# Attention and feed-forward kernel: the mark above a threshold as the upper byte of bf16, without the constant pass

## The chip, the cores and the metric

The kernel runs on one core of a Trainium2 chip. The metric is device time in microseconds (us) of that core for the whole program, the median of several runs. Engines are TensorE (PE, with PEld for its weight loads), VectorE (DVE), ScalarE (ACT), GpSimd (POOL) and SyncE (SP, which issues DMAs).

## What is computed

`x` has shape (16, 512, 256). The layer is attention with 16 heads of width 16, in which each row of scores keeps its 31 largest entries, then a layer norm, then a gated feed-forward layer of width 768 with integer weights, then a second layer norm. Cut to what matters:

```python
scores = einsum('bhqd,bhkd->bhqk', Q, K) / sqrt(16)
top_vals, _ = top_k(scores, 31)
scores = where(scores < top_vals[..., -1:], -inf, scores)
context = einsum('bhqk,bhkd->bhqd', softmax(scores), V)
x = layernorm(x + context @ Wo.T + bo)
h = silu(x @ wg.T) * (x @ wu.T)
x = layernorm(x + h @ wd.T)
```

## The kernel before, in words

The work goes batch by batch, and within a batch in 64 slots. A slot is one tile of scores, 128 queries of one head against 512 keys. Every engine has its own program, `slots`, which runs over n = 0 to 63 and does in slot n one step of each of several tiles at once; constants at the head of the file say how many slots behind the scores a step runs (`COUNT0 = 1`, `COUNT1 = 2`, `BELOW = 4`, `BLOCK = 5`, `SORT = 6`, `PICK = 14`, `THRESHOLD = 16`, `MASK = 17`, `TURNED = 23`, `EXPO = 24`, `PV = 25`, `GROUP = 41`). Semaphores tie the programs together. The loop is unrolled over batches, five or seven at a time; what a batch adds (projections, feed-forward and so on) has fixed slots: `HALF_USES` for the projections and statistics, `VALUES_AT` 4 and 26, `OUT_PROJ` 30 and 31, `FFN_SLOTS` 43 to 54, `DOWN_SLOTS` 58 to 61. These use two PSUM tiles, `bench`.

The steps of one tile are these.

- TensorE computes the scores into `S_ps` (L604). Keys and queries are kept as a high and a low part, so this is a matmul over 64 rows.
- VectorE copies them to `S`, shifted by a first estimate of the threshold, and takes the row maximum (L870, `evacuate`).
- ScalarE counts how many entries lie above that estimate, smoothly (L469, `count_first`), and corrects the estimate with the count. It then takes the sign of each entry against the second estimate, writes it to `above` and sums it to `s1` (L479, `count_second`). The sign is -1, 0 or 1, as bf16.
- TensorE (`below`, L614, L615, L617) builds in `Y_ps` the scores with all entries above the second estimate pushed out of sight. `nbig` is the identity times -BIG, BIG = 2^40. The first matmul writes nbig x `ones_b`, that is -2^40 everywhere. The second adds nbig x `above`, so that the sum is 0 where the sign is -1, and -2^41 where it is 1. The third adds the scores again.
- VectorE finds the eight largest of each of four blocks of `Y_ps` (L877), sorts them (L890 to L897), and for every eight tiles (a "pair" of heads) picks by the count in `s1` the one that has rank 31 (`pick`, `pick_candidate`, `pick_threshold`). `flag` tells which rows of which tile may be wrong. TensorE sums the flags over the rows (L660, `sum_flags`, with the column of ones `onesc`), ScalarE copies the sums as integers (L458), and VectorE reads them (`check`) and runs a full search (`general`, L940 and L944) where one is not zero.
- GpSimd makes the mask from `S` and the threshold (L1109, `cut`), with a shift `mb` by the row maximum over BIG.
- TensorE computes the scores again, transposed, and adds nbig x mask (L628, L631, `turned`); ScalarE takes the exponential to `PT` (L487); TensorE multiplies by the values (L645, `values`).

Buffers that matter here: `S_ps` and `Y_ps` have two places each, `ST_ps` one, `above` and `PT` four. TensorE starts `below` when `cnt1_done` says that `above` is written and `blocks_done` that the tile two before has been read. ScalarE waits before it writes `above` for `below_done` of four tiles before.

In the prologue VectorE sets constants (L1059 to L1066), waits for ten loads, converts `ident` and `heads` (L1068, L1069), makes `nbig` (L1070) and raises `consts_done`, for which TensorE's first projection (L558) waits.

Of the kernel before, what the change touches and what calls it, by code (L numbers as in the profile page):

```python
# [8 lines left out]
B, L, DM = 16, 512, 256  # L9
# [3 lines left out]
P = 128  # L13
# [10 lines left out]
SCALE = float(D) ** -0.5  # L24
DEQ = float(np.float32(1.0 / 127.0))
EPS = 1e-5
GONE = -3.0e38
BIG = 2.0 ** 40

# [10 lines left out]
BLOCKS = 4  # L42
BW = L // BLOCKS
RANKS = 16
TINY = 1.0e-30


COUNT0 = 1
# [19 lines left out]
PAIR = 2 * NT  # L68
# [18 lines left out]
F32R = mybir.dt.float32r  # L87
I32 = mybir.dt.int32
BF16 = mybir.dt.bfloat16
ALU = mybir.AluOpType  # L90
ACT = mybir.ActivationFunctionType
AX = mybir.AxisListType
# [29 lines left out]
def score_place(j):  # L122

    return (j, 22) if j < 21 else (j - 21, 21) if j < 42 else (j - 42, 21 if j < 63 else 64)
# [36 lines left out]
def tile_place(part):  # L161
    return part % 2, part // 2


def build(nc, xT, x, wqT, wkT, wvT, woT, bq, bk, bv, bo, wgT, wuT, wdT, ident_in, blocks_in, heads_in, ranks_in, out):
    with ExitStack() as ctx:
        def sb(name, shape, dt=F32):
            return ctx.enter_context(nc.sbuf_tensor(name, shape, dt))

        def ps(name, shape):  # L170
            return ctx.enter_context(nc.psum_tensor(name, shape, F32))

        def sem(name):
            return ctx.enter_context(nc.semaphore(name))

        ident = sb("ident", [P, P])
        ident_r = sb("ident_r", [P, P], F32R)
        nbig = sb("nbig", [P, P], BF16)
        ones_b = sb("ones_b", [P, L], BF16)
        blk = sb("blk", [P, P])  # L180
        heads = sb("heads", [P, HALF])
        heads_r = sb("heads_r", [P, HALF], F32R)
        ranks = sb("ranks", [P, RANKS])
        ones = sb("ones", [1, P])
        ones_3 = sb("ones_3", [3, P], BF16)
        onesc = sb("onesc", [P, 1])
        wqk = [sb(f"w{n}", [P, C, DM]) for n in "qk"]
        bqk = [sb(f"b{n}", [P, 2]) for n in "qk"]
        wv = sb("wv", [P, C, DM])
# [2 lines left out]
        brow = sb("brow", [1, DM])  # L192
        bparts = [sb(f"bpart{i}", [1, DM], BF16) for i in range(3)]
        brows = sb("brows", [3, DM], BF16)
        wg = sb("wg", [P, C, HID], F32R)
# [11 lines left out]
        ksums = sb("ksums", [P, HALF], F32R)  # L207
        Kn = sb("Kn", [P, NT, P], BF16)
        gram = sb("gram", [P, P], F32R)
# [33 lines left out]
        S = sb("S", [P, S_PLACES, L])  # L243
# [5 lines left out]
        s0 = sb("s0", [P, 8])  # L249
        above = sb("above", [P, 4, L], BF16)  # L250
# [5 lines left out]
        picked = sb("picked", [P, PAIR, RANKS])  # L256
        least = sb("least", [P, PAIR])
        hidden = sb("hidden", [P, PAIR])
        flag = sb("flag", [P, 2, PAIR + 1])
        flag_i = sb("flag_i", [1, 2, 16], I32)  # L260
        W = sb("W", [P, L])
        gtop = sb("gtop", [P, 4, 8])
# [1 line left out]
        PT = sb("PT", [P, 4, L])  # L264
# [3 lines left out]
        ST_ps = ps("ST_ps", [P, L])  # L268
# [8 lines left out]
        consts_done = sem("consts_done")  # L277
# [24 lines left out]
        exp_done = sem("exp_done")  # L302
# [32 lines left out]
        def wait_apart(eng, s, value):  # L335
            eng.wait_ge(s, value)
            eng.nop(nofuse=True)
# [71 lines left out]
        def _(act):  # L409
# [63 lines left out]
            def count_second(T, n, first):  # L473
                j = (n - COUNT1) % TILES
                hb, col = j // HALF_TILES, (j % NT) * HALF + j // NT % HALF
                act.wait_ge(cnt0_done, T - COUNT1 + 1)
                if not (first and n < COUNT1 + 4):
                    act.wait_ge(below_done, T - COUNT1 - 3)
                nc.scalar.activation(above[:, j % 4, :], S[:, score_place(j)[0], :], ACT.Sign, bias=s0[:, j % 8:j % 8 + 1],  # L479
                                     scale=steep[:, hb, col:col + 1], accum_out=s1[:, j % RING:j % RING + 1]).then_inc(cnt1_done, 1)  # L480

            def exponentials(T, n, first):
                j = (n - EXPO) % TILES
                act.wait_ge(st_done, T - EXPO + 1)
                if not (first and n < EXPO + 4):
                    act.wait_ge(pv_done, T - EXPO - 3)
                nc.scalar.activation(PT[:, j % 4, :], ST_ps[:, :], ACT.Exp, scale=SCALE).then_inc(exp_done, 1)  # L487

            def normalised(b, i, tiles, done):
                act.wait_ge(mrstd_done, (b - 1) * 4 + 2 * i + 2)  # L490
# [4 lines left out]
            def slots(b, first, rest, finish):  # L495
                for n in range(TILES):
# [6 lines left out]
                    if due(EXPO, n, first, rest):  # L503
                        exponentials(T, n, first)
# [27 lines left out]
                    if due(COUNT1, n, first, rest):  # L532
                        count_second(T, n, first)
# [21 lines left out]
        def _(pe):  # L555
# [37 lines left out]
            def stacks(h):  # L593

                return h // 2, slice(h % 2 * 4 * D, (h % 2 + 1) * 4 * D)
# [11 lines left out]
            def below(T, n, first):  # L607
                j = (n - BELOW) % TILES
                (r, rows), q = stacks(j // NT), j % NT * P
                Y = Y_ps[j % 2]  # L610
                pe.wait_ge(cnt1_done, T - BELOW + 1)
                if not (first and n < BELOW + 2):
                    pe.wait_ge(blocks_done, T - BELOW - 1)
                nc.tensor.matmul(Y[:, :], nbig[:, :], ones_b[:, :], start=True, stop=False)  # L614
                nc.tensor.matmul(Y[:, :], nbig[:, :], above[:, j % 4, :], start=False, stop=False)  # L615

                nc.tensor.matmul(Y[:, :], QS[rows, r, q:q + P], KS[rows, r, :], start=False, stop=True,  # L617
                                 tile_position=(rows.start, 0)).then_inc(below_done, 1)
# [167 lines left out]
            for c in range(C):  # L786
                nc.tensor.matmul(bench[0][0:1, 0:DM], bvc[:, c:c + 1], wo[:, c, :], start=(c == 0), stop=False)
            nc.tensor.matmul(bench[0][0:1, 0:DM], ones[:, 0:1], brow[:, :],
                             start=False, stop=True).then_inc(brow_done, 1)
# [8 lines left out]
        def _(dve):  # L798
            steps = [0]

            def mark(ins):
                ins.then_inc(dve_step, 1)
                steps[0] += 1
                return steps[0]

            def split_low(what, hb, splits, at):
                k, use = at
                dve.wait_ge(ready[k], use + 1)
                dve.wait_ge(hi_done, splits)
                if what:  # L810
                    mark(nc.vector.tensor_scalar(ksums[:, :], heads[:, :], ksum[:, :], None, ALU.mult))
                nc.vector.scalar_tensor_tensor(out=lo[what][:, :], in0=bench[k][:, :], scalar=bqk[what][:, hb:hb + 1],
                                               in1=hi[what][:, :].bitcast(F32),
                                               op0=ALU.add, op1=ALU.subtract).then_inc(lo_done, 1)
                dve.wait_ge(lo_done, splits)
                dve.nop(nofuse=True).then_inc(taken[k], 1)

            def head_gram(at):
                k, use = at
                dve.wait_ge(ready[k], use + 1)  # L820
                nc.vector.tensor_tensor(gram[:, :], bench[k][:, 0:P], blk[:, :], ALU.mult).then_inc(taken[k], 1)

            def quadratic_terms(at):
                k, use = at
                dve.wait_ge(ready[k], use + 1)
                nc.vector.tensor_tensor(quad[:, :], bench[k][:, :], hi[0][:, :].bitcast(F32),
                                        ALU.mult).then_inc(taken[k], 1)

            def moments(part, at):
                n = NT * HALF  # L830
                if part == 0:
                    k, use = at
                    dve.wait_ge(ready[k], use + 1)
                    m = mark(nc.vector.tensor_scalar(nmean[:, :], bench[k][:, n:2 * n], -1.0 / L, None, ALU.mult))
                    dve.wait_ge(dve_step, m)
                    m = mark(nc.vector.scalar_tensor_tensor(out=msq[:, :], in0=bench[k][:, n:2 * n], scalar=1.0 / L,
                                                            in1=nmean[:, :], op0=ALU.mult, op1=ALU.mult))
                    dve.wait_ge(dve_step, m)
# [4 lines left out]
                if part == 1:  # L843
                    m = mark(nc.vector.tensor_scalar(varc[:, :], var[:, :], TINY, None, ALU.max))
                    dve.wait_ge(dve_step, m)
# [213 lines left out]
            nc.vector.memset(V[:, :, :, :], 0.0).then_inc(dve_step, 1)  # L1059
            dve.wait_ge(dve_step, 1)  # L1060
            nc.vector.memset(V[:, :, :, 0:HG * VW].rearrange("p n g (h v) -> p n g h v", h=HG)[:, :, :, :, D:VW], 1.0)
            nc.vector.memset(ones_b[:, :], 1.0)
            nc.vector.memset(onesc[:, :], 1.0)
            nc.vector.memset(at_zero[:, :], -STEEP * (ZERO - Z))
            nc.vector.memset(ones[:, :], 1.0)
# [1 line left out]
            dve.wait_ge(w_loaded, 16 * N_W)  # L1067
            nc.vector.tensor_copy(ident_r[:, :], ident[:, :])  # L1068
            nc.vector.tensor_copy(heads_r[:, :], heads[:, :])  # L1069
            nc.vector.tensor_scalar(nbig[:, :], ident[:, :], -BIG, None, ALU.mult).then_inc(consts_done, 1)  # L1070
            split_low(0, 0, 1, tile_place(0))
            split_low(1, 0, 2, tile_place(1))
            head_gram(tile_place(3))
# [19 lines left out]
        def _(pool):  # L1093
            def cut(b, T, n, first):
                j = (n - MASK) % TILES
                h, t, r = j // NT, j % NT, j % RING
                if j % PAIR == 0:

                    pair = b * NP + (n - MASK) // PAIR
                    wait_apart(pool, thr_done, pair + 1)  # L1100
                    nc.gpsimd.tensor_scalar(rbig[:, :], rmax[:, r:r + PAIR], 1.0 / BIG, None, ALU.mult).then_inc(mb_done, 1)  # L1101
                    wait_apart(pool, mb_done, 2 * pair + 1)
# [9 lines left out]
            def first_thresholds(G, hb):  # L1112
# [7 lines left out]
                wait_apart(pool, stat_step, n0 + 4)  # L1120
                nc.gpsimd.tensor_scalar(back[:, hb, :], na[:, hb, :], -1.0 / BIG, None, ALU.mult).then_inc(stat_done, 1)

# [77 lines left out]
```

## Time and profile before

| | |
|---|---|
| median of 3 runs | 3109.65 us (3107.92 to 3110.01) |
| the profiled execution | 3103.19 us, span 3101.4 us |
| mean granted TensorE clock | 0.949 of 2.4 GHz |
| busy: PE, PEld | 2755.7 us, 1508.1 us |
| busy: DVE, ACT, POOL | 2498.1, 2498.3, 2401.1 us |
| HBM | 20.86 MB read, 8.39 MB written |

The span is the time between the first and the last instruction of one execution that the hardware profiler recorded. Busy times are sums over that span. A matmul's recorded time includes its passage through the array, and the next one starts before it ends, so recorded times of TensorE overlap. The granted clock is the share of full speed that TensorE was given; it has two levels, 1.2 and 2.4 GHz, so a mean of 0.949 is a tenth of the time at the lower one.

### The profile page before, as it was taken

To read this page: it belongs to the slowest core of one execution; us is meant where nothing else is said; L and a number is where in the kernel's file an instruction comes from. 1 tells how busy PE (TensorE), PEld (TensorE's weight loads), DVE (VectorE), ACT (ScalarE), POOL (GpSimd) and SP (SyncE) were. 2 spreads that over 40 slices of the span, in tenths; PEclk is the share of its full clock that TensorE was granted. 3 is DMA by queue.
4 is the path that set the end of the run, shared out by engine and by line. 5 is a ranking of instruction groups with operands and counts; after the bars stand their busy time and mean duration, and the time that the engine had idled before them with its cause. 6 is when DMAs were issued, how large, how long until landed. Compare 5 with 4: busy or idle time off the path is not lost.

```text
span 3101.4 us, 81062 instructions
## 1 busy us (share of the span) xinstructions
PE 2755.7 (89%) x21030; PEld 1508.1 (49%) x21375; DVE 2498.1 (81%) x12298; ACT 2498.3 (81%) x5894; POOL 2401.1 (77%) x1677
## 2 busy tenths in 40 slices
PE   4988999999998998899999998999989998999986
PEld 2444544555454554544545454454545544454554
DVE  4888888888888878888888888878888888888861
ACT  4888888888888877788888888878878887888862
POOL 1887887788888876788788787877878787788882
PEclk7889999999999999999999999999999999999987
DMA  3201011120111101011010111102011020111000
GB/s 84 50 18 44 21 49 29 27 45 22 41 25 40 37 22 41 19 42 37 24 45 25 38 27 38 38 21 46 21 38 35 24 46 25 36 29 30 21 15 7
DMA packets 91143, 102.64 MB, mean 33 GB/s; under 512 B 34513, under 2 KB 52946, under 8 KB 90578
## 3 DMA queue, kind: packets, MB, share of 16 engines
q1 hardware_dynamic: 88544, 93.73, 12.7%
q8 instruction: 185, 3.03, 0.4%
q14 instruction: 380, 3.11, 0.3%
q10 hardware_dynamic: 2034, 2.76, 0.3%
HBM read 20.86 MB, written 8.39 MB: 9 GB/s over the span
## 4 chain that ended last, share of the span: by engine, by line
PE 53%; ACT 19%; issue 13%; DVE 11%; SPq 1%; POOL 1%; ACTq 1%; DVEq 1%; DMA 0%; POOLq 0%
ACT junk L469 8%; PE Y_ps L617 6%; PE ST_ps L628 6%; PE ST_ps L631 6%; PE ctxT_ps L645 6%; PE bench L681 6%; PE bench L687 6%; ACT above L479 4%; ACT PT L487 4%; PE Y_ps L615 4%; DVE cand L877 4%; PE bench L558 4%; PE Y_ps L614 3%; PE bench L674 2%; PE bench L589 2%
## 5 line engine op out<-in xcount | busy, mean ns | idle before, releaser
L1109 POOL TENSOR_SCALAR mask<-S,thr,mb 128x512 bf16<-128x512 f32 x1024 | 2113.6, 2076 | 43.0 <-POOL mb L1103 35.8
L877 DVE MAX8 cand<-Y_ps 128x8 f32<-128x128 f32 x4096 | 1069.7, 281 | 6.5 <-issue 6.4
L870 DVE TENSOR_SCALAR_CACHE_REDUCE S<-S_ps,na 128x512 f32<-128x512 f32 x1024 | 756.7, 739 | 320.4 <-PE S_ps L604 257.5
L469 ACT ACTIVATE junk<-S,at_zero,slope 128x512 bf16<-128x512 f32 x1024 | 827.1, 808 | 160.1 <-DVE S L870 155.6
L479 ACT ACTIVATE above<-S,s,steep 128x512 bf16<-128x512 f32 x1024 | 823.0, 804 | 0.0
L487 ACT ACTIVATE PT<-ST_ps 128x512 f32<-128x512 f32 x1024 | 596.0, 582 | 190.3 <-PE ST_ps L631 189.2
L628 PE MATMUL ST_ps<-QS,KS 64*128 64x512 f32 x1024 | 466.8, 456 | 130.0 <-ACT PT L487 126.9
L604 PE MATMUL S_ps<-KS,QS 64*128 64x512 f32 x1024 | 524.6, 513 | 4.2 <-DMA KS<-Klo 2.2
L617 PE MATMUL Y_ps<-KS,QS 64*128 64x512 f32 x1024 | 524.7, 512 | 1.2 <-issue 1.1
L615 PE MATMUL Y_ps<-above,nbig 128*128 128x512 bf16 x1020 | 400.1, 392 | 69.5 <-DVE cand L877 36.9
L631 PE MATMUL ST_ps<-nbig,mask 128*128 128x128 bf16 x4096 | 420.6, 227 | 0.0
L617 PEld LDWEIGHTS Y_ps<-KS,QS 64*128 64x128 f32 x1024 | 192.7, 188 | 458.0 <-issue 458.0
L1101 POOL TENSOR_SCALAR rbig<-rmax 128x8 f32<-128x8 f32 x128 | 31.1, 243 | 478.5 <-DVEq L964 478.5
L631 PEld LDWEIGHTS ST_ps<-nbig,mask 128*128 128x128 bf16 x4096 | 239.0, 100 | 319.6 <-issue 319.6
L645 PE MATMUL ctxT_ps<-PT,V 128*32 128x128 f32 x8192 | 349.8, 291 | 0.0
L614 PE MATMUL Y_ps<-ones_b,nbig 128*128 128x512 bf16 x683 | 273.7, 401 | 82.9 <-DVE cand L877 69.4
L628 PEld LDWEIGHTS ST_ps<-QS,KS 64*128 64x128 f32 x1024 | 196.8, 192 | 270.0 <-ACT PT L487 250.4
L645 PEld LDWEIGHTS ctxT_ps<-PT,V 128*32 128x32 f32 x8192 | 202.7, 113 | 58.8 <-issue 8.6
L890 DVE MAX8 best<-cand 128x8 f32<-128x32 f32 x1024 | 191.9, 187 | 40.0 <-issue 35.5
L614 PEld LDWEIGHTS Y_ps<-ones_b,nbig 128*128 128x128 bf16 x1024 | 100.5, 98 | 226.5 <-issue 169.7
L469 ACT ACTIVATION_READ_ACCUMULATOR junk<-S,at_zero,slope 128x1 f32 x1024 | 196.2, 192 | 0.0
L479 ACT ACTIVATION_READ_ACCUMULATOR above<-S,s,steep 128x1 f32 x1024 | 195.7, 191 | 0.0
(125 smaller groups left out, 3661.6 us busy)
## 6 DMA issues: line engine op xcount, KB each, us to landing
QS<-Qhi SPq DMA_DIRECT2D x512, 32.0 KB, 2.0
KS<-Khi SPq DMA_DIRECT2D x512, 32.0 KB, 2.0
KS<-Klo SPq DMA_DIRECT2D x512, 32.0 KB, 2.0
QS<-Qlo SPq DMA_DIRECT2D x512, 32.0 KB, 2.0
xTs<-in_xT SPq DMA_DIRECT2D x17, 512.0 KB, 3.7
xs<-in_x SPq DMA_DIRECT2D x16, 512.0 KB, 3.9
out<-xs SPq DMA_DIRECT2D x16, 512.0 KB, 2.9
hT<-in_wgT ACTq DMA_DIRECT2D x1, 768.0 KB
```

The source lines that it names most:

```text
L469: nc.scalar.activation(junk[:, :], S[:, score_place(j)[0], :], ACT.Tanh, bias=at_zero[:, :], scale=slope[:, hb, col:col + 1], accum_out=s0 ...
L479: nc.scalar.activation(above[:, j % 4, :], S[:, score_place(j)[0], :], ACT.Sign, bias=s0[:, j % 8:j % 8 + 1], scale=steep[:, hb, col:col + ...
L487: nc.scalar.activation(PT[:, j % 4, :], ST_ps[:, :], ACT.Exp, scale=SCALE).then_inc(exp_done, 1)
L604: nc.tensor.matmul(S_ps[n % 2][:, :], QS[rows, r, q:q + P], KS[rows, r, :], start=True, stop=True, tile_position=(rows.start, 0)).then_inc ...
L615: nc.tensor.matmul(Y[:, :], nbig[:, :], above[:, j % 4, :], start=False, stop=False)
L617: nc.tensor.matmul(Y[:, :], QS[rows, r, q:q + P], KS[rows, r, :], start=False, stop=True, tile_position=(rows.start, 0)).then_inc(below_do ...
L628: nc.tensor.matmul(ST_ps[:, :], KS[rows, r, kt * P:(kt + 1) * P], QS[rows, r, :], start=True, stop=False, tile_position=(rows.start, 0))
L631: mm = nc.tensor.matmul(ST_ps[:, t * P:(t + 1) * P], mask[:, h % MASKS, t, kt * P:(kt + 1) * P], nbig[:, :], start=False, stop=(t == NT - 1))
L645: mm = nc.tensor.matmul(ctxT_ps[32 * a:32 * a + 32, strip * P:(strip + 1) * P], V[:, k, grp, strip * VW:strip * VW + 32], PT[:, (j - kt + ...
L870: nc.vector.tensor_scalar(S[:, at, :], S_ps[n % 2][:, :], na[:, hb, col:col + 1], None, ALU.add, op1=ALU.max, accum_out=rmax[:, n % RING:n ...
L877: mx = nc.vector.max(cand[:, j % CANDS, i, :], Y_ps[j % 2][:, i * BW:(i + 1) * BW])
L1109: nc.gpsimd.tensor_scalar(mask[:, h % MASKS, t, :], S[:, score_place(j)[0], :], thr[:, r:r + 1], mb[:, r:r + 1], ALU.is_lt, op1=ALU.add).t ...
```

## The change

The sign is written as one byte, into the upper byte of each bf16 of `above`, whose lower bytes are 0 from a memset in the prologue. A byte of 1 there is the bf16 number 2^-125; -1 and 0 are to become the byte 0, which is the number 0. `nbyte`, the identity times -2^127, brings this to -4 or 0 in one matmul, so the constant matmul and `ones_b` go. The 4 has to be far above the scores, so the key weights and biases are multiplied by 2^-38 in the prologue, which makes every score smaller by that power of two; BIG becomes 4, the floor `TINY` of the variance is lowered, and the exponential's scale is divided by 2^-38. Flags and their column of ones are bf16.

```diff
-BIG = 2.0 ** 40
+SHIFT = 2.0 ** -38
+BIG = 4.0
+BYTE_BIG = 2.0 ** 127
...
-TINY = 1.0e-30
+TINY = 1.0e-36
...
-        ones_b = sb("ones_b", [P, L], BF16)
+        nbyte = sb("nbyte", [P, P], BF16)
...
-        onesc = sb("onesc", [P, 1])
+        onesc = sb("onesc", [P, 1], BF16)
...
-        flag = sb("flag", [P, 2, PAIR + 1])
+        flag = sb("flag", [P, 2, PAIR + 1], BF16)
...
-                nc.scalar.activation(above[:, j % 4, :], S[:, score_place(j)[0], :], ACT.Sign, bias=s0[:, j % 8:j % 8 + 1],
+                nc.scalar.activation(above[:, j % 4, :].bitcast(U8).rearrange("p (l y) -> p l y", y=2)[:, :, 1], S[:, score_place(j)[0], :], ACT.Sign, bias=s0[:, j % 8:j % 8 + 1],
                                      scale=steep[:, hb, col:col + 1], accum_out=s1[:, j % RING:j % RING + 1]).then_inc(cnt1_done, 1)
...
-                nc.scalar.activation(PT[:, j % 4, :], ST_ps[:, :], ACT.Exp, scale=SCALE).then_inc(exp_done, 1)
+                nc.scalar.activation(PT[:, j % 4, :], ST_ps[:, :], ACT.Exp, scale=SCALE / SHIFT).then_inc(exp_done, 1)
...
-                nc.tensor.matmul(Y[:, :], nbig[:, :], ones_b[:, :], start=True, stop=False)
-                nc.tensor.matmul(Y[:, :], nbig[:, :], above[:, j % 4, :], start=False, stop=False)
+                nc.tensor.matmul(Y[:, :], nbyte[:, :], above[:, j % 4, :], start=True, stop=False)
...
-            nc.vector.memset(ones_b[:, :], 1.0)
+            nc.vector.memset(above[:, :, :], 0.0)
...
-            nc.vector.tensor_scalar(nbig[:, :], ident[:, :], -BIG, None, ALU.mult).then_inc(consts_done, 1)
+            nc.vector.tensor_scalar(nbig[:, :], ident[:, :], -BIG, None, ALU.mult)
+            nc.vector.tensor_scalar(nbyte[:, :], ident[:, :], -BYTE_BIG, None, ALU.mult)
+            nc.vector.tensor_scalar(bqk[1][:, :], bqk[1][:, :], SHIFT, None, ALU.mult)
+            nc.vector.tensor_scalar(wqk[1][:, :, :], wqk[1][:, :, :], SHIFT, None, ALU.mult).then_inc(consts_done, 1)
+            dve.wait_ge(consts_done, 1)
```

## Rows read from the trace of the kernel before

**Rows 1.** Page, busy time of each engine, and the granted clock in 40 slices:
```profile
PE 2755.7 (89%) x21030; PEld 1508.1 (49%) x21375; DVE 2498.1 (81%) x12298; ACT 2498.3 (81%) x5894; POOL 2401.1 (77%) x1677
...
PEclk7889999999999999999999999999999999999987
```

**Rows 2.** Page, chain that ended last, by engine, then by line:
```profile
PE 53%; ACT 19%; issue 13%; DVE 11%; SPq 1%; POOL 1%; ACTq 1%; DVEq 1%; DMA 0%; POOLq 0%
ACT junk L469 8%; PE Y_ps L617 6%; PE ST_ps L628 6%; PE ST_ps L631 6%; PE ctxT_ps L645 6%; PE bench L681 6%; PE bench L687 6%; ACT above L479 4%; ACT PT L487 4%; PE Y_ps L615 4%; DVE cand L877 4%; PE bench L558 4%; PE Y_ps L614 3%; PE bench L674 2%; PE bench L589 2%
```

**Rows 3.** Page, costliest groups: busy us, mean ns | idle before, releaser:
```profile
L870 DVE TENSOR_SCALAR_CACHE_REDUCE S<-S_ps,na 128x512 f32<-128x512 f32 x1024 | 756.7, 739 | 320.4 <-PE S_ps L604 257.5
...
L479 ACT ACTIVATE above<-S,s,steep 128x512 bf16<-128x512 f32 x1024 | 823.0, 804 | 0.0
L487 ACT ACTIVATE PT<-ST_ps 128x512 f32<-128x512 f32 x1024 | 596.0, 582 | 190.3 <-PE ST_ps L631 189.2
...
L614 PE MATMUL Y_ps<-ones_b,nbig 128*128 128x512 bf16 x683 | 273.7, 401 | 82.9 <-DVE cand L877 69.4
```

**Rows 4.** Timeline of TensorE: start us, us, what:
```profile
1524.95 0.38 PE L614 MATMUL Y_ps<-ones_b,nbig 128*128 128x512 bf16 x1
1525.16 0.38 PE L615 MATMUL Y_ps<-above,nbig 128*128 128x512 bf16 x1
```

**Rows 5.** Windows, one batch each: length, busy (instructions) by engine, PEclk, DMA share, GB/s:
```profile
745.15:929.12 183.97, 167.84 (x1314) 92.18 (x1336) 154.98 (x766) 155.65 (x368) 149.12 (x104) 0.98 0.14 33
929.12:1115.75 186.63, 169.27 (x1314) 93.26 (x1336) 154.20 (x766) 157.28 (x372) 149.47 (x105) 0.97 0.14 33
1115.75:1315.59 199.84, 175.31 (x1312) 95.24 (x1335) 164.22 (x786) 154.66 (x364) 149.14 (x103) 0.92 0.13 31
1499.48:1680.27 180.79, 165.18 (x1315) 91.00 (x1336) 154.27 (x766) 155.00 (x368) 149.21 (x104) 1.00 0.14 34
```

**Rows 6.** Windows, the batch from 1499.48 by slots 0, 11, 18, 26, 34, 57:
```profile
1499.48:1527.82 28.34, 23.82 (x218) 12.43 (x220) 22.74 (x124) 26.13 (x64) 21.27 (x15) 1.00 0.12 39
1527.82:1546.47 18.65, 18.02 (x136) 9.24 (x139) 16.82 (x84) 16.47 (x41) 14.86 (x8) 1.00 0.11 25
1546.47:1565.56 19.09, 16.17 (x143) 7.81 (x144) 18.06 (x101) 17.48 (x43) 18.19 (x15) 1.00 0.24 52
1565.56:1591.00 25.44, 24.26 (x186) 13.55 (x188) 18.88 (x94) 19.46 (x47) 17.40 (x13) 1.00 0.21 51
1591.00:1656.37 65.37, 59.99 (x481) 32.92 (x488) 57.77 (x276) 60.77 (x143) 59.80 (x39) 1.00 0.15 34
1656.37:1680.27 23.90, 22.94 (x163) 15.05 (x165) 20.00 (x91) 14.70 (x35) 17.69 (x17) 1.00 0.01 2
```

**Rows 7.** Timeline of TensorE, one sum of flags (two matmuls):
```profile
1500.93 0.20 PE L660 MATMUL bench<-flag,onesc 128*1 128x9 f32 x2
```

**Rows 8.** Groups by form, ScalarE's copies `Kn` and `V`:
```profile
L448 ACT ACTIVATE V<-bench 128x256 f32<-128x256 f32 x64 | 21.2, 383 | 51.1 <-PE bench L589 51.1
...
L439 ACT ACTIVATE Kn<-bench 128x512 bf16<-128x512 f32 x33 | 19.3, 583 | 1.0 <-PE bench L564 1.0
```

**Rows 9.** Timeline of the prologue, VectorE and TensorE:
```profile
14.68 0.23 DVE L1068 CAST ident_r<-ident 128x128 fp32r<-128x128 f32 x1 [11.40 <-DMA bvc<-in_bv]
...
14.89 0.22 DVE L1070 TENSOR_SCALAR nbig<-ident 128x128 bf16<-128x128 f32 x1
...
15.17 3.78 PE L558 MATMUL bench<-xTs,wq 128*128 128x512 f32 x4 [15.17 <-DVE nbig L1070]
```

**Rows 10.** Windows, weak stretches and the low clock behind one; one more fall:
```profile
1549.00:1558.00 9.00, 6.66 (x53) 3.04 (x56) 8.61 (x49) 7.44 (x18) 9.00 (x6) 1.00 0.24 53
1729.50:1739.40 9.90, 6.76 (x50) 3.13 (x50) 9.15 (x48) 7.50 (x19) 9.74 (x8) 1.00 0.23 50
1739.40:1742.80 3.40, 3.40 (x26) 1.42 (x24) 2.85 (x14) 2.95 (x8) 3.24 (x5) 0.50 0.25 55
...
1838.40:1841.80 3.40, 3.40 (x14) 1.85 (x13) 2.53 (x14) 2.73 (x8) 0.44 (x2) 0.50 0.01 2
```

More of the change, by code:

```diff
@@ L89 @@
 BF16 = mybir.dt.bfloat16
+U8 = mybir.dt.uint8
 ALU = mybir.AluOpType
```

## The prediction

> **What bounds the kernel now.** I read the page's busy lines first. TensorE is busy 2755.7 of 3101.4 us, VectorE and ScalarE some 2498 each, GpSimd 2401; the granted clock is 9 tenths nearly throughout, so short falls are spread over the whole run [rows 1]. So TensorE leads, but three others stand within 13% of it. The chain that ended last says how much of that lead is on the path: 53% of the span is TensorE's, 19% ScalarE's, 11% VectorE's, and the line the change deletes, the constant pass L614, has 3%, the pass on `above` L615 4% [rows 2]. Then the groups by line: the constant pass is listed with 401 ns each (683 of its 1024 records are there) [rows 3]. These times overlap: the reader should look at starts. The constant pass starts at 1524.95 and the pass on `above` at 1525.16 [rows 4]. So a pass of 512 columns holds TensorE for about 0.22 us, and not for the 0.40 that is listed, by which the removed work would be 411 us in all.
>
> A batch is 64 slots. The batch from 1499.48 to 1680.27 takes 180.79 us at full clock. Others take 183.97 and 186.63 with 0.98 and 0.97 granted, and one with 0.92 takes 199.84 [rows 5] (in that one VectorE also runs two full searches of a row, lines 940 and 944). The undisturbed batch, cut into six stretches, shows where TensorE is the bound [rows 6]. In slots 11 to 17 (18.65 us), 26 to 33 (25.44 us) and 57 to 63 (23.90 us) it is busy over 95% and the next engine stands well below. In slots 0 to 10 ScalarE leads (26.13 of 28.34), in 18 to 25 GpSimd and VectorE do (18.19 and 18.06 of 19.09), and in 34 to 56 ScalarE, TensorE and GpSimd are level (60.77, 59.99, 59.80 of 65.37).
>
> **The change part by part.**
>
> *The constant pass goes* (1024 matmuls and 1024 weight loads). TensorE does 1024 x 0.22 = 225 us less. What of it comes off the end is bounded from above by the chain: 3% of 3101.4 us, 93 us, or 5.7 us a batch. From below I take the stretches of rows 6, with 0.22 us a slot removed and stopped by the next engine:
> - slots 0 to 10: 2.4 us removed, ScalarE already leads; 0.3 us gained
> - slots 11 to 17: 1.5 us removed, VectorE has 16.82 of 18.65 and is soon full; 0.9 us
> - slots 18 to 25: 0.2 us
> - slots 26 to 33: 1.8 us removed, the next engine has 19.46 of 25.44; 1.4 us
> - slots 34 to 56: 5.1 us removed, three engines level, only the slots with a feed-forward matmul gain; 0.9 us
> - slots 57 to 63: 1.5 us removed, VectorE has 20.00 of 23.90; 1.1 us
>
> That is 4.8 us a batch, **-77 us** over 16. If only the three stretches led by TensorE gave, it would be 3.4 x 16 = -54 us; the chain's own bound is -93 us. The sum takes the middle, since it is what each stretch has room for.
>
> *The flags as bf16.* L660 now issues two matmuls for each of 128 sums, 172 ns each, the pair 0.20 us [rows 7], and one after. What is saved lies between 0.03 us (0.20 less 0.17) and a whole 0.17 us, half of the 128 on the path: between -2 and -11 us. I take **-3 us**, near the lower end, because the pair overlaps almost whole. VectorE writes 8 small flags in either type: nothing.
>
> *ScalarE writes bytes.* L479 writes every second byte instead of 512 bf16 values. No row has a byte output. The nearest ones say that neither width nor stride of the output counts: 128x512 to bf16 takes 583 ns (`Kn`), to f32 582 (`PT`, [rows 3]); 128x256 written in strides into `V` takes 383 [rows 8], less than the contiguous 512 elements. So 0. The other end: if each byte write cost a second access, 512 elements would add what 256 do twice, 2 x (583 - 383) = 400 ns; this end is a rival below. On the low side, a faster write: those same rows exclude it.
>
> *The scaling by a power of two* leaves every instruction of the loop as it was: the same copies, the same exponential with another constant, the same masks. Only the prologue grows: a memset of `above` four times the size of the one it replaces, ahead of VectorE's 11.40 us wait for loads and covered by it (without that cover it would cost a us or two); and three operations ahead of `consts_done`, which the first matmul waits for at 15.17 us [rows 9]. `nbyte` is 0.22 as `nbig`, the bias at most that, the key weights (128x512 f32) between 0.22 and the 0.74 of the evacuation L870 [rows 3]: **+1 us**, fully on the path.
>
> *The clock.* This is where the gain can be given back. The granted clock falls from 2.4 to 1.2 GHz for a few us where TensorE had just been less busy. In slots 19 to 22 TensorE was busy 6.66 of 9.00 us (74%) in the undisturbed batch, and the clock stayed. In the next batch it was busy 6.76 of 9.90 us (68%) there, and the clock was 0.50 in the following 3.40 us, in which TensorE was busy all through; it fell so too near slot 56, at 1838.40 [rows 10], and elsewhere near slots 2 and 38. Three or four passes less in such a stretch are 0.7 to 0.9 us: from 6.66 of 9.00 to below 5.96, 66%. The first kind becomes the second. The low time of a batch follows from its clock: 2 x (1 - 0.98) x 184 = 7.4 us, 11.2 us at 0.97, 32 at 0.92, none at 1.00, 12.6 us in the mean of the four. Its price is (183.97 - 180.79)/7.4 = 0.43 and (186.63 - 180.79)/11.2 = 0.52 us per us [rows 5]. I estimate half as much low time again, 6 us a batch, at 0.4 (TensorE has less to catch up): 2.4 us a batch, **+37 us** over 15.5 batches. Bounds: no more falls, 0; or 15 us more a batch at 0.45, +105 us. I stay nearer the lower end, since the better part of a batch is 90% busy and keeps a margin.
> The Trainium skill (TensorE: Matmul & The Clock Gate, Part 1) states that the throttled clock is the default and that activity releases it. The trace agrees, by the 0.50 behind the weaker stretch, and by that rule work taken from an engine that already waits is no pure gain: if it decides, the second rival comes.
>
> **Sum.** -77 - 3 + 1 + 37 = -42 us. The profiled execution took 3103.19 us (span 3101.4), the runs' median is 3109.65, 6.5 us more. I carry the difference over: 3109.65 - 42 = 3068 us.
>
> **The rivals.**
> 1. *No extra falls.* The gain stays whole: -77 - 3 + 1 = -79, so 3031 us. For it: where slots get shorter, TensorE's busy share hardly drops. Against it: the weak stretch is paced by GpSimd (9.00 of 9.00) and VectorE (8.61 [rows 10]), which do not speed up.
> 2. *The clock costs more than the pass did.* At each of the weak places of a batch (about slots 2, 22, 38 and 56) the clock falls nearly every time, and at one of them for several times 3.4 us: 15 us more a batch, +105 us against -79: +26, 3136 us. It decides from about 11 us more low time a batch (79/15.5/0.45). For it: the work removed exceeds the difference between the stretch that fell and the one that stayed [rows 10]. Against it: low time costs less where TensorE has slack.
> 3. *The other engines absorb it.* Only the -54 of the lower bound and the same +37 remain, with VectorE's and ScalarE's waits on each other in place of those on TensorE: -19 to 0, some 3100 us.
> 4. *Byte writes are slow.* ScalarE gains 0.4 us a slot, 2498 + 410 = 2908 us of work, and leads everywhere: its 19% of the chain [rows 2] becomes most of it. With its idle time taken up partly, some +250 us, 3360 us.
> 5. *The change doesn't do what it says.* Were -1 to become another byte than 0, everything would be hidden and VectorE's full search, two rows in a rare batch now, would run in all of them: many times the time. Nothing in the trace can show the conversion.
>
> **How the numbers follow.** Forecast 0.42, no extra falls 0.24, clock costs more 0.20, absorbed 0.09, slow bytes 0.03, wrong bytes 0.02. Predicted 3068 us; its own range is 3043 to 3093 (some 15 us either way for the pass, inside -54 to -93, and 20 for the clock, seldom both at once). The range for 8 in 10 runs from 3018 to 3138: below it lies the full chain bound, above it the upper half of rival 2 and rivals 4 and 5. A measurement of this kernel can tell 0.2%, 6 us, from no change. Faster: nearly all of the forecast and rival 1 and a little of rival 3, 0.67. Within: 0.09. Slower: the rest, 0.24.
>
> **What would show it.** Right: L614 gone; L617 starting 0.2 us earlier behind `cnt1`; batches at clock 1.00 near 176 us; VectorE's wait for the scores (L870) and ScalarE's for the transposed scores below before; mean clock near 0.93. Each step: L479 still 804 ns [rows 3]; L660 x128; the first matmul at about 16.2 us. Wrong: L479 over 850 ns; a mean clock still 0.95 (rival 1) or under 0.91 (rival 2); undisturbed batches over 178 us (rival 3); more than a few `gtop` rows (rival 5).

## The result, and the profile after

The changed kernel takes 3142.71 us in the median of 4 runs (3127.95 to 3156.49), the kernel before 3108.78 us in 4 runs. The ratio is 1.0112, with a 95% interval of 1.0063 to 1.0161: slower by 1.1%, where 1.3% faster was forecast. It lies above the range of 3018 to 3138 us. The case that came is the second rival, "the clock costs more than the pass did", which gave 3136 us.

The page of the changed kernel, busy time and granted clock (answers to [rows 1]):

```profile
PE 2688.8 (86%) x19924; PEld 1531.2 (49%) x20223; DVE 2495.7 (80%) x12301; ACT 2501.1 (80%) x5894; POOL 2402.3 (77%) x1677
...
PEclk7888979889998988889989998998979988898977
```

TensorE has 67 us less busy time, although 225 us of passes are gone, and the clock shows 8 in nearly half of the slices where it was 9. The mean granted clock of the profiled execution (3138.8 us, span 3137.0) is 0.887, against 0.949. As low time that is 2 x (1 - 0.887) x 3137 = 709 us at 1.2 GHz, against 316 us: 393 us more. The chain that ended last, by engine and by line (answers to [rows 2]):

```profile
PE 47%; ACT 18%; issue 15%; DVE 14%; POOL 2%; SPq 1%; DVEq 1%; ACTq 1%; DMA 0%; POOLq 0%
ACT junk L474 7%; PE ctxT_ps L649 6%; PE ST_ps L632 6%; PE Y_ps L621 6%; PE bench L685 6%; PE ST_ps L635 6%; PE bench L691 5%; DVE cand L881 5%; ACT PT L492 4%; ACT above L484 4%; PE Y_ps L619 3%; PE bench L563 3%; PE bench L594 2%; PE bench L678 2%; DVE S L874 2%
```

TensorE went from 53% to 47% of it. The deleted line had 3% of that. VectorE went from 11% to 14%, "issue" from 13% to 15% and GpSimd from 1% to 2%. The groups by line, busy us, mean ns | idle before and its releaser (answers to [rows 3]):

```profile
L874 DVE TENSOR_SCALAR_CACHE_REDUCE S<-S_ps,na 128x512 f32<-128x512 f32 x1024 | 757.8, 740 | 340.7 <-PE S_ps L609 285.1
...
L484 ACT ACTIVATE above<-S,s,steep 128x512 uint8<-128x512 f32 x1024 | 825.6, 806 | 0.0
L492 ACT ACTIVATE PT<-ST_ps 128x512 f32<-128x512 f32 x1024 | 596.1, 582 | 174.9 <-PE ST_ps L635 173.6
...
L619 PE MATMUL Y_ps<-above,nbyte 128*128 128x512 bf16 x725 | 312.7, 431 | 77.8 <-DVE cand L881 63.5
```

ScalarE's pass with byte output takes 806 ns, 2 more than before. VectorE did not wait less for the scores but more (285.1 against 257.5 us), although TensorE has one matmul less in front of them. The pass on `above`, now the first of its group, is listed with 431 ns, where the first of before had 401 [rows 3]. The unchanged matmul of the scores grew by the same 30 ns (L604, now L609, from 513 to 543): a fifth of the time is now at the low clock. The waits themselves, us in total, times, longest, and below them TensorE's wait of the kernel before:

```profile
DVE S L874 <- PE S_ps L609: 285.1, 249, 4.5
PE ST_ps L632 <- ACT PT L492: 214.2, 390, 1.3
ACT PT L492 <- PE ST_ps L635: 173.6, 119, 5.8
```

```profile
PE ST_ps L628 <- ACT PT L487: 126.9, 246, 1.2
```

Of these only ScalarE's wait for the transposed scores went down, from 189.2 to 173.6 us. TensorE's own wait for the exponential grew from 126.9 to 214.2 us: a good part of the time it was given went there. Five batches of 64 slots, by length, busy time, clock, DMA share and GB/s (answers to [rows 5]; the fourth is the one with two full searches):

```profile
383.01:570.86 187.85, 166.36 (x1246) 95.29 (x1264) 154.79 (x765) 155.90 (x368) 149.14 (x105) 0.89 0.13 33
758.83:943.25 184.42, 161.13 (x1245) 92.56 (x1264) 154.07 (x765) 155.76 (x368) 149.36 (x105) 0.94 0.14 33
943.25:1129.58 186.33, 162.40 (x1245) 92.95 (x1263) 153.87 (x766) 157.38 (x372) 149.61 (x106) 0.93 0.14 33
1129.58:1332.97 203.39, 175.97 (x1246) 100.19 (x1264) 163.26 (x785) 154.89 (x365) 149.08 (x103) 0.83 0.13 30
1520.07:1707.78 187.71, 167.24 (x1246) 95.53 (x1264) 154.96 (x765) 155.51 (x367) 149.12 (x105) 0.88 0.14 33
```

No batch runs at 1.00 any more. The second to the fifth have 22, 26, 69 and 45 us of low time; the same four batches of before had 7, 11, 32 and 0 [rows 5]. The places are much the same in every batch: slots 0 to 4, 18 to 26 and 37 to 39 above all. Here are three stretches ahead of a fall, each with the low stretch behind it; the first fall is a long one that held from slot 18 to 26 (answers to [rows 10]):

```profile
430.00:433.90 3.90, 3.70 (x35) 2.30 (x36) 3.72 (x21) 3.44 (x10) 1.22 (x3) 1.00 0.25 56
433.90:457.80 23.90, 22.10 (x143) 11.21 (x138) 20.70 (x107) 18.63 (x45) 20.37 (x17) 0.50 0.24 52
487.00:492.00 5.00, 3.05 (x31) 1.57 (x32) 4.67 (x23) 4.64 (x11) 4.63 (x5) 1.00 0.18 39
492.00:498.80 6.80, 6.49 (x37) 3.56 (x37) 4.30 (x24) 5.39 (x14) 6.80 (x5) 0.50 0.21 47
570.86:577.30 6.44, 3.50 (x35) 1.87 (x35) 5.46 (x31) 5.42 (x14) 2.91 (x5) 1.00 0.01 3
577.30:587.50 10.20, 10.16 (x65) 6.35 (x66) 6.30 (x34) 7.35 (x17) 9.94 (x5) 0.50 0.32 104
```

In front of the second and third fall TensorE was busy 61% and 54% of the time while ScalarE and VectorE were busy over 80%: it waits for them there, and a pass less makes it wait more. The long one does not fit this by its busy times: TensorE was busy 95% of the 3.9 us ahead of it, and 92% of the 23.9 us at half speed.

### The profile page after: what moved, and what is told of

It reads as the page before. It is cut to its first block, busy times and chain, and to the rows that moved or that the text cites. A ratio compares the mean times of both kernels' runs of the same rounds, so it can differ in the third digit from the quotient of the medians.

```text
span 3137.0 us, 78807 instructions
## 1 busy us (share of the span) xinstructions
PE 2688.8 (86%) x19924; PEld 1531.2 (49%) x20223; DVE 2495.7 (80%) x12301; ACT 2501.1 (80%) x5894; POOL 2402.3 (77%) x1677
## 4 chain that ended last, share of the span: by engine, by line
PE 47%; ACT 18%; issue 15%; DVE 14%; POOL 2%; SPq 1%; DVEq 1%; ACTq 1%; DMA 0%; POOLq 0%
ACT junk L474 7%; PE ctxT_ps L649 6%; PE ST_ps L632 6%; PE Y_ps L621 6%; PE bench L685 6%; PE ST_ps L635 6%; PE bench L691 5%; DVE cand L881 5%; ACT PT L492 4%; ACT above L484 4%; PE Y_ps L619 3%; PE bench L563 3%; PE bench L594 2%; PE bench L678 2%; DVE S L874 2%
## 5 line engine op out<-in xcount | busy, mean ns | idle before, releaser
L874 DVE TENSOR_SCALAR_CACHE_REDUCE S<-S_ps,na 128x512 f32<-128x512 f32 x1024 | 757.8, 740 | 340.7 <-PE S_ps L609 285.1
L484 ACT ACTIVATE above<-S,s,steep 128x512 uint8<-128x512 f32 x1024 | 825.6, 806 | 0.0
L492 ACT ACTIVATE PT<-ST_ps 128x512 f32<-128x512 f32 x1024 | 596.1, 582 | 174.9 <-PE ST_ps L635 173.6
L632 PE MATMUL ST_ps<-QS,KS 64*128 64x512 f32 x1024 | 501.8, 490 | 216.1 <-ACT PT L492 214.2
L621 PE MATMUL Y_ps<-KS,QS 64*128 64x512 f32 x1024 | 556.7, 544 | 94.5 <-DVE cand L881 35.7
L609 PE MATMUL S_ps<-KS,QS 64*128 64x512 f32 x1024 | 555.3, 543 | 4.2 <-DVE S L874 2.6
L635 PE MATMUL ST_ps<-nbig,mask 128*128 128x128 bf16 x4096 | 447.2, 238 | 0.0
L635 PEld LDWEIGHTS ST_ps<-nbig,mask 128*128 128x128 bf16 x4096 | 254.1, 104 | 344.1 <-issue 344.1
L619 PE MATMUL Y_ps<-above,nbyte 128*128 128x512 bf16 x725 | 312.7, 431 | 77.8 <-DVE cand L881 63.5
L649 PE MATMUL ctxT_ps<-PT,V 128*32 128x128 f32 x8192 | 379.1, 310 | 0.0
L619 PEld LDWEIGHTS Y_ps<-above,nbyte 128*128 128x128 bf16 x1024 | 104.1, 102 | 235.4 <-issue 172.7
L609 PEld LDWEIGHTS S_ps<-KS,QS 64*128 64x128 f32 x1024 | 203.5, 199 | 5.4 <-DVE S L874 3.7
```

The source lines that it names most:

```text
L484: nc.scalar.activation(above[:, j % 4, :].bitcast(U8).rearrange("p (l y) -> p l y", y=2)[:, :, 1], S[:, score_place(j)[0], :], ACT.Sign, b ...
L609: nc.tensor.matmul(S_ps[n % 2][:, :], QS[rows, r, q:q + P], KS[rows, r, :], start=True, stop=True, tile_position=(rows.start, 0)).then_inc ...
L619: nc.tensor.matmul(Y[:, :], nbyte[:, :], above[:, j % 4, :], start=True, stop=False)
L632: nc.tensor.matmul(ST_ps[:, :], KS[rows, r, kt * P:(kt + 1) * P], QS[rows, r, :], start=True, stop=False, tile_position=(rows.start, 0))
L635: mm = nc.tensor.matmul(ST_ps[:, t * P:(t + 1) * P], mask[:, h % MASKS, t, kt * P:(kt + 1) * P], nbig[:, :], start=False, stop=(t == NT - 1))
L649: mm = nc.tensor.matmul(ctxT_ps[32 * a:32 * a + 32, strip * P:(strip + 1) * P], V[:, k, grp, strip * VW:strip * VW + 32], PT[:, (j - kt + ...
```

## The experiments

"Useless matmuls" below are matmuls of 512 columns whose result nobody reads. In a free `bench` tile they are issued ahead of TensorE's wait for the exponential, where it often stands still. Where they or the constant pass come back into the changed kernel, `ones_b` and its memset come back too. No experiment leaves out a part of the computation.

**The pass given back, all else changed.**

```diff
+                nc.tensor.matmul(Y[:, :], nbyte[:, :], above[:, j % 4, :], start=True, stop=True)
                 nc.tensor.matmul(Y[:, :], nbyte[:, :], above[:, j % 4, :], start=True, stop=False)
```

> The changed kernel with its one pass on `above` issued twice (the first overwritten), so TensorE has as many matmuls as before the change, at the same place of the chain. Everything else of the change stays. Clock theory (the removed pass cost clock, the rest of the change costs nothing): back to the time of before, 3100 to 3115 us, mean clock 0.94 to 0.95. Rival (byte writes, scaling or bf16 flags cost something): stays above 3130 us, at whatever clock. Rival (the clock drops for another reason than the amount of matmul work): clock stays at 0.89.

Measured: 3112.48 us, ratio to before 1.0011 (0.9993 to 1.0029), clock 0.946. Its page, busy time and clock:

```profile
PE 2767.3 (89%) x20902; PEld 1509.0 (48%) x21247; DVE 2502.0 (80%) x12301; ACT 2501.3 (80%) x5894; POOL 2402.2 (77%) x1677
...
PEclk7899999999999999999999999999989999999987
```

So the kernel is back at the time of before with the byte writes, the scaling and the bf16 flags all in place. What made it slower is the missing matmul, and the lost clock came back with it. TensorE's wait for the exponential is 129.3 us again, where it was 126.9 and 214.2.

**The pass given back ahead of the wait.**

```diff
-                pe.wait_ge(cnt1_done, T - BELOW + 1)
                 if not (first and n < BELOW + 2):
                     pe.wait_ge(blocks_done, T - BELOW - 1)
+                nc.tensor.matmul(Y[:, :], nbig[:, :], ones_b[:, :], start=True, stop=True)
+                pe.wait_ge(cnt1_done, T - BELOW + 1)
```

> The changed kernel with a constant pass ahead of the wait for cnt1_done, which the pass on `above` then overwrites: same work for TensorE as before, but issued before ScalarE's result is there. Clock theory: clock 0.94 or 0.95, and a little faster than before, 3085 to 3110 us, since some of the passes now lie in waits. Rival (time is set by the number of instructions in the chain): about 3140 us.

Measured: 3108.15 us, 0.9984 (0.9969 to 1.0000), clock 0.945. Against the run above that is 4 us, and the intervals overlap: the place of the pass behind ScalarE's result is worth next to nothing.

**One useless matmul in 20 weak slots**, in the changed kernel and in the one before. The function is called in `turned`, ahead of the wait for `exp_done`; the wait on `taken` is the one that the tile's next user has anyway.

```diff
+WEAK = {n: m for m, ns in ((1, (0, 1, 2, 3, 16, 17, 18, 19, 20, 21, 22, 23, 28, 29, 35, 36, 37, 38, 62, 63)),) for n in ns}
...
+            def spare(b, n, first):
+                if first or n not in WEAK:
+                    return
+                have, last = [0, 0], [-9, -9]
+                for m in range(n):
+                    for use in uses_of(m, False, False):
+                        have[BANKS[m, use]] += 1
+                        last[BANKS[m, use]] = m
+                k = min((0, 1), key=lambda i: last[i])
+                if last[k] > n - 2:
+                    return
+                pe.wait_ge(taken[k], (b - 1) * BATCH_COUNT[k] + (PROLOGUE_COUNT[k] + FIRST_COUNT[k] + have[k]))
+                for _ in range(WEAK[n]):
+                    nc.tensor.matmul(bench[k][:, :], nbig[:, :], ones_b[:, :], start=True, stop=True)
```

> The changed kernel with one useless matmul of 512 columns into a free `bench` tile ahead of the wait for the exponential, in some 20 of 64 slots, those where the clock falls. Clock theory: mean clock 0.93 or more at a third of the work added back, so the pass's gain shows: 3050 to 3095 us, faster than before. Rival (the other engines absorb the gain whatever the clock): clock rises but the time stays at 3105 or more.

> The kernel before with the same useless matmuls in the same slots, nothing else changed. Clock theory: the low clock time of before also goes, mean clock 0.96 to 0.97, and at a price of 0.45 us per us of low time 3050 to 3095 us. Rival (the added work costs what it is): 10 to 50 us slower than before.

Measured: the changed kernel 3145.61 us, 1.0108 (1.0080 to 1.0137), clock 0.918; the kernel before 3088.71 us, 0.9936 (0.9916 to 0.9956), clock 0.965. The second is as expected. Adding 300 matmuls to a kernel led by TensorE made it 20 us faster, and its page shows the clock at 9 nearly everywhere:

```profile
PEclk7899999999999989999999999999999999999987
```

The first is a miss: the low time fell from 709 to 516 us and the time did not. Two of its batches, one without a fall and one with:

```profile
1715.17:1893.85 178.68, 158.87 (x1264) 89.64 (x1284) 154.43 (x765) 155.59 (x369) 149.52 (x105) 1.00 0.15 34
1524.98:1715.17 190.19, 169.74 (x1264) 96.06 (x1284) 154.94 (x765) 156.07 (x368) 149.07 (x105) 0.93 0.13 32
```

Without a fall the batch takes 178.68 us, the shortest undisturbed one so far. With 0.93 the other takes 190.19 us, more than the same batch of the changed kernel at 0.88 (187.71 us). A likely reason, not tested by itself, is that the added matmuls then stand in stretches that still fall, where each costs twice. Slots 18 to 25 of that batch, in the changed kernel and in this run, fit it: with less low time (14 us against 22) they take longer.

```profile
1569.07:1592.72 23.65, 21.62 (x134) 10.94 (x135) 20.13 (x108) 18.79 (x46) 19.02 (x18) 0.53 0.23 52
```

```profile
1573.86:1598.43 24.57, 21.47 (x140) 10.26 (x141) 20.17 (x105) 18.41 (x44) 18.82 (x18) 0.72 0.23 51
```

One matmul a slot was too little in slots 20 to 25, where 10 to 20 us of low time remained in most batches.

**More of them, chosen by where the clock still fell**, 38 a batch, in the changed kernel (the edit is shown against the first list).

```diff
-WEAK = {n: m for m, ns in ((1, (0, 1, 2, 3, 16, 17, 18, 19, 20, 21, 22, 23, 28, 29, 35, 36, 37, 38, 62, 63)),) for n in ns}
+WEAK = {n: m for m, ns in ((1, (0, 2, 17, 18, 19, 23, 28, 35, 40, 49, 62, 63)), (2, (1, 3, 20, 21, 22, 24, 25, 29, 36, 37, 38, 41, 56)),) for n in ns}
```

> The changed kernel with one or two useless matmuls into a free `bench` tile ahead of the wait for the exponential, in 25 slots chosen by where the clock still fell with one: slots 20 to 25 and 36 to 41 above all. Clock theory: mean clock 0.96 or more, undisturbed batches near 179 us, 3070 to 3095 us. Rival (useless matmuls cost in the chain what they bring): clock as said, time at 3110 us or more. The undisturbed batches also measure the pass itself: 176 us if it is worth the 4.8 us a batch of the prediction, 178 to 179 if 2.

Measured: 3084.46 us, 0.9916 (0.9892 to 0.9941). The clock of the profiled execution is 0.947, below the expected 0.96; that execution (span 3094.6 us) is at the slow end of the kernel's runs (3081.95 to 3096.46). An undisturbed batch, cut at the same slots as [rows 6]:

```profile
755.96:784.28 28.32, 23.31 (x209) 12.29 (x212) 23.37 (x124) 26.37 (x65) 21.79 (x16) 1.00 0.12 39
784.28:802.92 18.64, 17.13 (x131) 9.02 (x133) 16.61 (x84) 16.68 (x41) 14.75 (x8) 1.00 0.12 27
802.92:822.36 19.44, 17.70 (x146) 8.26 (x148) 17.89 (x100) 17.45 (x42) 18.51 (x16) 1.00 0.23 50
822.36:847.13 24.77, 23.32 (x179) 13.17 (x182) 18.58 (x95) 19.46 (x49) 16.85 (x11) 1.00 0.21 52
847.13:912.27 65.14, 58.91 (x467) 32.63 (x474) 58.02 (x278) 60.84 (x143) 60.14 (x40) 1.00 0.15 34
912.27:935.17 22.90, 22.46 (x158) 14.91 (x160) 19.52 (x90) 14.77 (x36) 17.73 (x17) 1.00 0.01 3
sum 179.21, PE 162.83 PEld 90.28 DVE 153.99 ACT 155.56 POOL 149.78; mean PE 27.14 PEld 15.05 DVE 25.66 ACT 25.93 POOL 24.96
```

The added group in the groups by form (its 555 records are 37 a batch in 15 batches, some are missing):

```profile
L639 PE MATMUL bench<-ones_b,nbig 128*128 128x512 bf16 x555 | 193.3, 402 | 5.2 <-issue 2.4 <-DVE x1T L1073 1.7
```

This batch bears on what the pass is worth at full clock, less what the added matmuls cost. It takes 179.21 us against 180.79, 1.6 less: slots 0 to 10 are unchanged (28.32 and 28.34), 11 to 17 too (18.64 and 18.65), though only one matmul was added in them; 18 to 25 are 0.35 longer, with the most added per slot; 26 to 33 give 0.67, 34 to 56 give 0.23, 57 to 63 give 1.00. It is not the same one of the 16 batches, though, and they differ at full clock too. The fair partner of the 178.68 us above is the same batch of the kernel before with the same 20 useless matmuls:

```profile
1679.73:1861.46 181.73, 172.39 (x1334) 93.30 (x1355) 154.85 (x764) 155.96 (x369) 149.12 (x105) 1.00 0.15 34
```

That is 3.05 us. So the pass is worth 1.6 to 3.1 us a batch, by what else TensorE is given to do. Two stretches of the changed kernel itself stayed at full clock, slots 11 to 17 in one batch and 57 to 63 in another; they took 18.65 and 23.90 us before [rows 6], 0.2 and 1.0 more:

```profile
1550.63:1569.07 18.44, 16.88 (x130) 8.96 (x132) 16.69 (x83) 16.47 (x40) 14.98 (x8) 1.00 0.11 24
...
1869.09:1891.95 22.86, 21.57 (x155) 14.61 (x157) 19.62 (x90) 15.24 (x36) 17.55 (x17) 1.00 0.01 2
```

**The constant pass twice in the kernel before**, the experiment in the other direction.

```diff
+                nc.tensor.matmul(Y[:, :], nbig[:, :], ones_b[:, :], start=True, stop=True)
                 nc.tensor.matmul(Y[:, :], nbig[:, :], ones_b[:, :], start=True, stop=False)
```

> The kernel before with the constant pass issued twice in each slot: 1024 matmuls, 225 us of TensorE work, more at the same place of the chain. Clock theory (work removed and clock lost about cancel): the low time goes down to a third of before, mean clock 0.97 or more, and the time moves by under 1.5%, 3100 to 3150 us. Rival (the pass's gross worth is the 77 us of the prediction and before had little clock to win): 3170 us or more.

Measured: 3125.30 us, 1.0051 (1.0034 to 1.0068), clock 0.972. Two undisturbed batches, and the clock of the page:

```profile
1510.09:1694.27 184.18, 175.50 (x1379) 96.35 (x1400) 154.11 (x764) 155.48 (x368) 149.34 (x105) 1.00 0.14 33
1879.30:2066.01 186.71, 176.05 (x1377) 96.39 (x1399) 154.39 (x764) 157.30 (x372) 149.46 (x105) 1.00 0.14 33
```

```profile
PEclk7999999999999999999999999999999999999987
```

At full clock, in the same batch, a pass more costs 184.18 - 180.79 = 3.4 us, 54 us in 16. The kernel lost 15 us. 225 us of additional TensorE work were paid for in good part by low time that went from 316 to 175 us, to over a half and not to the third that was expected.

**Early pass and useless matmuls together.** The changed kernel with the edit of the second experiment and the first list of 20 weak slots.

> The changed kernel with the constant pass ahead of the wait for cnt1_done in all slots, and one useless matmul in the 20 weak slots: TensorE has the work of the kernel before with the same useless matmuls (3089 us), but one pass less behind ScalarE's result. Clock theory: mean clock 0.96 to 0.97, 3075 to 3090 us. Rival (the place of the pass is worth nothing): 3089 us within 0.3%.

Measured: 3085.94 us, 0.9916 (0.9887 to 0.9944), clock 0.965. Against 0.9936 for the kernel before with the same useless matmuls the intervals overlap: again no more than a few us for the place of the pass.

**The flags alone**, in the kernel before: `onesc` and `flag` as bf16 and nothing else.

> The kernel before with flags and their column of ones as bf16, nothing else. By the prediction 3 us faster (2 to 11), not to be told from no change. Rival: these matmuls stand in weak stretches too, so the clock gets worse by some of it; then also within 0.2%.

Measured: 3109.60 us, 0.9995 (0.9979 to 1.0011), clock 0.946. Nothing that can be told from no change.

**The same number elsewhere, and a better choice**, both in the changed kernel. The first list has 38 useless matmuls where TensorE is busy anyway, the second 46 where it is not.

```diff
+WEAK = {n: m for m, ns in ((1, (5, 6, 7, 10, 11, 12, 13, 14, 27, 31)), (2, (15, 26, 30, 32, 33, 34, 42, 43, 45, 47, 50, 52, 54)), (1, (58, 59)),) for n in ns}
...
+WEAK = {n: m for m, ns in ((1, (0, 2, 4, 7, 8, 10, 17, 18, 19, 23, 28, 35, 40, 49, 62)), (2, (1, 3, 9, 20, 21, 24, 25, 29, 36, 37, 38, 41, 56, 63)), (3, (22,)),) for n in ns}
```

> The changed kernel with 38 useless matmuls a batch, as many as in the run that took 3084 us, but in the other slots, where TensorE is busy anyway (5 to 7, 10 to 15, 26 to 34, 42 to 59). Clock theory (it is where TensorE waits that the clock falls): mean clock 0.89 to 0.91, the falls at slots 18 to 26, 37 to 39 and 0 to 4 stay, 3140 us or more. Rival (the amount over a batch decides): clock 0.94 or more, under 3110 us.

> The changed kernel with useless matmuls in a few slots more than the run with 38 of them: also in slots 4 and 7 to 10, two in 9 and 63, three in 22, 46 in all a batch. Clock theory: fewer falls left at 2 to 4, 8 to 11 and 22 to 26, mean clock 0.955 to 0.97, 3070 to 3085 us. Rival (all that can be won is won): 3084 us within 0.3%.

Measured: elsewhere 3204.02 us, 1.0292 (1.0254 to 1.0330), clock 0.895. In the weak slots 3078.46 us, 0.9887 (0.9851 to 0.9923), clock 0.959. The page's clock and one batch of the first:

```profile
PEclk7888989989998998989989898999989988998977
```

```profile
580.28:774.33 194.05, 174.82 (x1280) 97.06 (x1302) 154.84 (x765) 156.14 (x368) 148.95 (x105) 0.90 0.13 32
```

and of the second, a batch without a fall:

```profile
PEclk7889999999999989999999999999989999999987
```

```profile
748.79:928.22 179.43, 164.85 (x1287) 90.87 (x1309) 154.22 (x766) 155.60 (x369) 149.59 (x104) 1.00 0.14 34
```

With as many matmuls in the busy slots the clock stays where the changed kernel had it, and the time is 61 us above the changed kernel's; in the weak slots 38 bring 58 us. What counts is where they stand. The tuned list makes the fastest kernel of this study, 1.1% faster than before and 64 us faster than the change alone.

## Why the prediction was wrong

The mechanism stood in it, as the clock term and as rival 2; the sizes of both large terms were off, the gain too large and the loss too small, and so the sign of the sum.

**The pass, -77 us: too large.** Measured at full clock it is 1.6 to 3.1 us a batch, 26 to 49 us, where 4.8 us and -77 were taken; even the low bound of -54 was too much. The step that failed is the gain by stretches. In the batch with 38 useless matmuls, slots 57 to 63 gave 1.00 of 1.1 us, 26 to 33 gave 0.67 of 1.4, 34 to 56 gave 0.23 of 0.9, and 0 to 10 nothing of 0.3. Slots 11 to 17 gave 0.2 of 0.9 in the changed kernel itself. The step took "TensorE is busiest here" as "TensorE sets the pace here". In slots 11 to 17 TensorE was 97% busy before and is 92% busy after, in 0.2 us less. The chain's 3% (93 us) was a true upper bound and a poor guide. Likely chains through ScalarE and VectorE run close behind it; no run isolates them. The same pass costs 3.4 us a batch when added.

**The clock, +37 us: too small.** More low time was right, and in the main the places. The reason given, that TensorE waits there, is borne out by the runs that add matmuls there or elsewhere, but not by the busy time ahead of the fall of 23.9 us. But it is 393 us, 25 a batch, where 6 was taken and 15 was the outer bound. I counted about one or two further falls of 3.4 us at the weak places. What came were long ones, 23.9 us in slots 18 to 26, 10 to 14 us at the batch change, and falls in every batch. The price was too high in turn: with 26 to 49 us gained by the pass and 34 us lost in sum, the clock cost 60 to 83 us, 0.15 to 0.21 us per us of low time, where I took 0.4. One cause is a reading of [rows 5]: the price of 0.52 sets unlike batches beside each other. With the pass twice, two such batches, both at 1.00, are 186.71 - 184.18 = 2.5 us apart, which leaves (186.63 - 180.79 - 2.5)/11.2 = 0.30. That a fall also costs less where TensorE has more slack is likely and not shown. In the sum the too small amount of low time weighed more than the too high price.

**The rest.** ScalarE's byte output costs 2 ns, as forecast. The conversion does what it says: full searches are four in both kernels. The flags, -3 us, are within what can't be told. Between VectorE's first conversion and the first matmul the prologue's three operations cost half of the +1 us. In the timeline of the changed kernel the first matmul follows `ident_r` by 15.16 - 14.13 = 1.03 us:

```profile
14.13 0.23 DVE L1072 CAST ident_r<-ident 128x128 fp32r<-128x128 f32 x1 [10.31 <-DMA bvc<-in_bv]
...
14.69 0.42 DVE L1077 TENSOR_SCALAR wk<-wk 128x512 f32<-128x512 f32 x1
...
15.16 3.78 PE L563 MATMUL bench<-xTs,wq 128*128 128x512 f32 x4 [15.16 <-DVE wk L1077]
```

Before, it was 15.17 - 14.68 = 0.49 us [rows 9]. The first matmul starts when it did, since in this execution VectorE's wait for the loads ended earlier.

**The rivals.** Rival 1 (no extra falls) fails by the clock. Rival 2 decided: its condition, 11 us more low time a batch, is far exceeded. That its 3136 us lies so near is luck: it had -79 and +105 us where the runs show -26 to -49 and +60 to +83. Part of rival 3 is true as well: the other engines took most of the pass's gain. Rivals 4 and 5 fail. The chances put 0.20 on rival 2, though the text named the fact that spoke for it, that the work removed exceeded the difference between the stretch that fell and the one that stayed. With the pass sized at 2 to 3 us a batch it decides from 10 to 15 us of low time even at a price of 0.2, and would have deserved more.

The Trainium skill (TensorE: Matmul & The Clock Gate, Part 1) says that activity releases the throttle. Here that held in a kernel whose TensorE is busy 86% of the span, in the mean granted clock of every run in which matmuls were added at the weak places or taken away: 0.887 without the pass, 0.949 with it, 0.972 with it twice. The 23.9 us at 0.50 in which TensorE was busy 92% of the time do not follow from it.

Open stays why a fall lasts 3.4 us in one batch and 23.9 in another, why that one came behind a busy stretch, and why the first list of 20 slots did not help the changed kernel, when it helped the kernel before.

## What to carry to other kernels

A matmul taken out of the chain is worth only what the other engines leave, and here it lowered TensorE's clock, since it stood where TensorE already waits. Look for the granted clock by stretch and not only in the mean, and cost removed work twice: once at full clock, once as low time. Compare a batch only with the same batch of the other kernel: batches at full clock differed by up to 2.5 us here, about what the pass is worth. Where a weak stretch can't be filled with useful work, useless matmuls ahead of a wait can pay; here they did so only in that stretch.

## What the runs showed that was not expected

A kernel led by TensorE got 0.6% faster by some 300 useless matmuls (3088.71 against 3109.20 us), and the changed kernel with 690 of them, in the right slots, is 1.1% faster than the kernel before (3078.46 us). 1024 matmuls more at the same place cost 0.5% in one direction, 1024 less cost 1.1% in the other. The clock held at 1.2 GHz for 23.9 us although TensorE was busy for 22.1 of them.
